# Selective scan: B and C rows repeated over the partitions by DMA instead of by TensorE, the scan's state in a PSUM bank, each product right behind its scan

## The reference, cut to what matters

```python
xn = _layer_norm(x, ln_g, ln_b)
xz = xn @ W_in.T;  u, z = xz[..., :DIN], xz[..., DIN:]
u = silu(causal_conv4(u) + conv_b)
dbc = u @ W_x.T                      # 8 columns dt_in, 16 columns B, 16 columns C
dt = softplus(dt_in @ W_dt.T + dt_bias)
dA  = exp(dt[..., None] * A)                      # decays
dBu = dt[..., None] * Bm[:, :, None, :] * u[..., None]
h = da * h + dbu;   y = einsum('bdn,bn->bd', h, c)   # for each position in turn
y = (y + u * D) * silu(z);   out = x + y @ W_out.T
```

## Time and profile before

| | |
|---|---|
| median of three runs | 1602.35 us (1600.36 to 1602.57) |
| profiled execution, its own time | 1599.76 us |
| span of its instructions | 1598.0 us |
| PE busy | 1340.2 us, 84% |
| DVE busy | 954.8 us, 60% |
| ACT busy | 699.1 us, 44% |
| POOL busy | 408.9 us, 26% |
| granted TensorE clock, mean | 0.934 of 2.4 GHz |

### The profile page before, as it was taken

The page is one execution under the profiler, slowest core; times in us unless marked ns, Lnnn a source line. Parts: engine busy times, 40 slices in busy tenths (PEclk is TensorE's granted clock), DMA queues, the critical chain, the costliest instruction groups (busy, mean ns, idle before and its releaser), DMA issues.

```text
span 1598.0 us, 24645 instructions
## 1 busy us (share of the span) xinstructions
PE 1340.2 (84%) x9074; PEld 852.2 (53%) x9127; DVE 954.8 (60%) x2239; ACT 699.1 (44%) x1988; POOL 408.9 (26%) x353
## 2 busy tenths in 40 slices
PE   7999767887887777868976468899898999999997
PEld 4666543555555433424544245555566566556664
DVE  2556667666663577685768777655674555643334
ACT  4555323456555566642645015522244555422222
POOL 1233004444431277655200224100100333400000
PEclk9999979999998889787999779999999999999999
DMA  9000000000000500000000000000000000000000
GB/s 382 1 1 1 1 1 1 1 1 1 1 1 1 212 1 1 1 0 1 2 1 0 0 0 2 1 1 0 1 2 2 1 1 1 1 1 1 0 0 13
DMA packets 4222, 25.69 MB, mean 16 GB/s; under 512 B 1168, under 2 KB 3216, under 8 KB 3472
## 3 DMA queue, kind: packets, MB, share of 16 engines
q1 hardware_dynamic: 4112, 24.24, 3.7%
HBM read 23.71 MB, written 0.52 MB: 15 GB/s over the span
## 4 chain that ended last, share of the span: by engine, by line
PE 43%; DVE 9%; issue 2%; ACT 2%; POOL 0%; DVEq 0%; ACTq 0%; POOLq 0%
PE PS L1071 6%; PE PS L641 6%; PE PS L1056 5%; PE PS L1057 5%; PE PS L707 3%; PE PS L325 2%; PE PS L357 2%; PE PS L337 2%; PE PS L298 1%; PE PS L306 1%; PE PS L1060 1%; PE PS L631 1%; PE PS L635 1%; DVE arena L877 1%; PE PS L366 1%
## 5 line engine op out<-in xcount | busy, mean ns | idle before, releaser
L549 POOL TENSOR_TENSOR arena<-arena,small 128x768 f32<-128x768 f32 (+1 forms) x64 | 107.7, 1683 | 225.3 <-DVE small L492 116.3
L877 DVE TENSOR_REDUCE arena<-PS 128x2 f32<-128x512 f32 (+1 forms) x192 | 108.9, 609 | 56.5 <-PE PS L635 55.5
L804 ACT ACTIVATE arena<-PS 128x512 f32<-128x512 f32 (+1 forms) x192 | 92.2, 532 | 109.0 <-PE PS L641 109.0
L1160 DVE TENSOR_TENSOR arena<-arena,PS 128x512 f32<-128x512 f32 x82 | 56.4, 688 | 115.9 <-ACT arena L1093 115.8
L1093 ACT ACTIVATE arena<-PS 128x512 f32<-128x512 f32 x82 | 49.0, 597 | 166.0 <-PE PS L1057 166.0
L641 PE MATMUL PS<-arena 32*128 32x256 f32 (+1 forms) x768 | 99.4, 376 | 13.6 <-DVE arena L877 9.3
L429 ACT ACTIVATE arena<-PS,small 128x256 f32<-128x256 f32 (+1 forms) x256 | 110.6, 452 | 0.0
L635 PE MATMUL PS<-arena 32*128 32x256 f32 (+1 forms) x768 | 96.6, 378 | 2.2 <-DVE arena L877 1.6
L2103 DVE TENSOR_TENSOR_SCAN arena<-PS,arena 128x512 f32<-128x512 f32 x64 | 78.1, 1222 | 27.8 <-ACT PS L2006 16.5
L2155 POOL TENSOR_TENSOR arena<-arena 128x512 f32<-128x512 f32 x64 | 80.2, 1269 | 52.6 <-ACT arena L1997 46.0
L500 DVE COPY arena<-PS 128x768 f32<-128x768 f32 (+1 forms) x64 | 69.5, 1086 | 34.5 <-PE PS L337 34.5
(11 more groups left out here) (407 smaller groups left out, 3118.4 us busy)
## 6 DMA issues: line engine op xcount, KB each, us to landing
w_last<-in_last SPq DMA_DIRECT2D x1, 8260.0 KB, 22.9
w_rest<-in_rest SPq DMA_DIRECT2D x1, 6533.5 KB, 37.2
w_last<-in_first SPq DMA_DIRECT2D x1, 4532.5 KB, 21.1
w_last<-in_first SPq DMA_DIRECT2D x1, 2176.0 KB, 10.2
X<-in_x SPq DMA_DIRECT2D x1, 512.0 KB, 4.4
CT<-in_ctxT SPq DMA_DIRECT2D x1, 512.0 KB, 10.8
out<-X SPq DMA_DIRECT2D x1, 512.0 KB, 3.2
w_consts<-in_consts SPq DMA_DIRECT2D x1, 373.0 KB, 3.1
```

The lines of the kernel that those rows point to most:

```text
L549: g.tensor_tensor(p, p, ri, ALU.mult).then_inc(self.pn_done.sem, 1)
L804: a.activation(self.PT[:, q % 8, :], PS[:, 3 + q % 3, 0:2 * n], ACT.Exp).then_inc(self.e_done.sem, 1)
L877: v.tensor_reduce(dst, src, AX.X, ALU.max, negate=True).then_inc(self.mx_done.sem, 1)
```

## The change

B and C are no longer repeated by PE. ACT's copy of dbc (now 40 rows: 32 of B and C, 8 of dt) is stored by SP to a DRAM tensor `rows`, and SP loads it back repeated over 128 partitions, two states of B and two of C in one DMA of 512 KB, into a ring of four slots in SBUF. `parts`, `spread_b`, `spread_c` and `b_copy` are gone. The banks that this frees become a fourth bank of decays (5) and the one bank of states (4). DVE does outputs(g) directly after scan(g), and scan(g) waits for outputs(g - 1). `logs` is split into `softening` (Abs, Relu, Exp; after n = 10) and `logs` (Ln; after n = 12); selections, steps, chain, gate, outputs and finish move a step or so earlier, and `dtu` has two buffers. For batch 0 the transposes of tiles 2 to 7 and their two copies come behind selections, and two table loads are issued ahead of need. The last layer's weights are loaded after the ring's last DMA. 34 products of zeros instead of 20 stand ahead of the stage. Cut to its core (declarations, the renumbered weight rows and the dropped one-hot table are left out):

```diff
-            keep_warm(self.c, pe, self.spare, 20)
+            keep_warm(self.c, pe, self.spare, 34)
...
-        return self.c.PS[:, (2, 3, 7)[g % 3], :]
+        return self.c.PS[:, (2, 3, 7, 5)[g % 4], :]
+    def state(self, g):
+        return self.c.PS[:, 4, :]
+    def spread(self, g, which):
+        return self.ring[:, g // 2 % self.RING, which * 2 + g % 2, :].unsqueeze(1).to_broadcast([P, 2, 256])
+    def out_bank(self, b):
+        return 1 if b + 1 < B else 6
...  # PE
-            if b:
-                pe.wait_ge(self.rl_ready.sem, self.rl_ready.at(0, b))
+            if b >= 2:
+                pe.wait_ge(self.z_ready.sem, self.z_ready.at(b - 2, 1))
...
-        transposes(2, 4, 5)
+        keep_warm(c, pe, 7, 3)
+        selections(0)
+        transposes(2, 4, 6)
         transposes(6, 2, 4)
-        selections(0)
-        keep_warm(c, pe, 3, 4)
         steps(0)
-        keep_warm(c, pe, 3, 16)
-        for g in range(5):
-            spread_b(g)
+        keep_warm(c, pe, 0, 24)
         for i in range(self.G):
             b, n = divmod(i, self.N)
-            spread_c(i)
             if i:
                 add(i - 1)
-            if i + 5 < self.G:
-                spread_b(i + 5)
-            if b and n == 3:
+            if b and n == 2:
                 outputs(b - 1)
...
+                if n == 6:
+                    selections(b + 1)
                 if n == 7:
-                    selections(b + 1)
-                if n == 8:
                     steps(b + 1)
...  # ACT
-            if g >= 3:
-                a.wait_ge(self.sc_ready.sem, self.sc_ready.at(0, g - 2))
+            if g >= 4:
+                a.wait_ge(self.sc_ready.sem, self.sc_ready.at(0, g - 3))
...
         silus(0)
-        normal(1, 5, 1, 2)
+        selections(0)
+        a.preload_act_table(ACT.Exp)
+        softening(0)
+        logs(0)
+        a.preload_act_table(ACT.Exp)
+        normal(1, 6, 1, 2)
         normal(2, 4, 3, 1)
-        selections(0)
-        logs(0)
-        b_copy(0)
-        b_copy(1)
         for g in range(self.G):
             decays(g)
-            if g + 2 < self.G:
-                b_copy(g + 2)
                 if n == 7:
                     silus(b + 1)
-                if n == 9:
+                if n == 8:
                     selections(b + 1)
-                if n == 11:
+                if n == 10:
+                    softening(b + 1)
+                if n == 12:
                     logs(b + 1)
...  # DVE
-            if g >= 2:
-                v.wait_ge(self.hc_ready.sem, self.hc_ready.at(0, g - 1))
-            v.tensor_tensor_scan(self.h[:, g % 2, :], self.decay(g), self.dB[:, g % 4, :], 0.0,
+            if g:
+                v.wait_ge(self.hc_ready.sem, self.hc_ready.at(0, g))
+            v.tensor_tensor_scan(self.state(g), self.decay(g), self.dB[:, g % 4, :], 0.0,
...
-            v.wait_ge(self.c_done.sem, self.c_done.at(0, g + 1))
-            v.tensor_tensor(two(self.hC[:, g % 3, :]), two(self.h[:, g % 2, :]),
-                            PS[:, 4, 0:256].unsqueeze(1).to_broadcast([P, 2, 256]), ALU.mult)\
+            v.tensor_tensor(two(self.hC[:, g % 3, :]), two(self.state(g)), self.spread(g, 1), ALU.mult)\
...
             scan(g)
-            if g:
-                outputs(g - 1)
-            if b and n == 1:
+            outputs(g)
+            if b and n == 0:
                 gate(b - 1)
-            if b and n == 4:
+            if b and n == 3:
                 finish(b - 1)
...  # POOL
-            g.wait_ge(self.bs_ready.sem, self.bs_ready.at(0, k + 1))
+            if k % 2 == 0:
+                g.wait_ge(slot.sem, slot.at(k // 2 // self.RING, 16))
...
-        self.parts(g, 0)
                 if n == 12:
-                    self.parts(g, b + 1)
-                if n == 13:
                     self.chain(g, b + 1, 0)
                     self.chain(g, b + 1, 1)
+                if n == 13:
+                    self.chain(g, b + 1, 2)
                 if n == 14:
-                    self.chain(g, b + 1, 2)
-                if n == 15:
                     self.chain(g, b + 1, 3)
                     self.chain(g, b + 1, 4)
...  # SP, ahead of the load of w_last
+    def sync(self, sp):
+        for k in range(self.G // 2):
+            b, m = divmod(k, self.N // 2)
+            if m == 0:
+                sp.wait_ge(self.dc_ev.sem, self.dc_ev.at(0, b + 1))
+                sp.dma_start(self.rows[b], self.DBC[0:32, b % 2, :]).then_inc(self.rows_out.sem, 16)
+                sp.wait_ge(self.rows_out.sem, self.rows_out.at(b, 16))
+            if k >= self.RING:
+                sp.wait_ge(self.hc_ready.sem, self.hc_ready.at(0, 2 * (k - self.RING) + 2))
+            rows = self.rows[b].rearrange("(w n) s -> w n s", w=2)[:, 2 * m:2 * m + 2, :]
+            sp.dma_start(self.ring[:, k % self.RING, :, :].rearrange("p (w n) s -> p w n s", w=2), rows.partition_broadcast(P))\
+                .then_inc(self.bc_in[k % self.RING].sem, 16)
```

More of the change, by code:

```diff
@@ L1774, with __init__ @@
     G = 16 * B
-    def __init__(self, c, g, b, win, cwb, cb, wdbc, wdt, bdt, alog, Ddiag, wout, onehot):
+    RING = 4
+    def __init__(self, c, g, b, win, cwb, cb, wdbc, wdt, bdt, alog, Ddiag, wout, rows):
         self.c, self.g, self.b, self.win, self.cb = c, g, b, win, cb
@@ L1779, in __init__ @@
         self.wdbc, self.wdt, self.bdt, self.alog, self.Ddiag = wdbc, wdt, bdt, alog, Ddiag
-        self.wout, self.onehot = wout, onehot
+        self.wout, self.rows = wout, rows
         self.x_tile = c.x_tile
@@ L1788, in __init__ @@
         self.dc_done, self.dc_ev = s("dc_done", B, 1), s("dc_ev", B, 1)
-        self.part_step = s("part_step", 7 * B, 1)
+        self.rows_out = s("rows_out", 16, B)
+        self.bc_in = [s(f"bc_in{k}", 16, len(range(k, G // 2, self.RING))) for k in range(self.RING)]
         self.dt_done, self.ab_ready, self.rl_ready = s("dt_done", B, 1), s("ab_ready", B, 1), s("rl_ready", B, 1)
@@ L1913, in tensor @@
         transposes(0, 2, 4)
-        for bank in (2, 3, 7):
+        for bank in (2, 3, 7, 5):
             keep_warm(c, pe, bank, 1)
@@ L1989, in logs @@
             a.activation(self.ex, self.ab, ACT.Exp, scale=-1.0).then_inc(self.ex_ready.sem, 1)
+        def logs(b):
             a.wait_ge(self.ex_ready.sem, self.ex_ready.at(0, b + 1))
             a.activation(self.lw, self.ex, ACT.Ln, bias=c.one, scale=1.0).then_inc(self.lw_ready.sem, 1)
[L1993 to L1997 removed]
         def decays(g):
@@ L2050, in chain @@
             eng.wait_ge(self.us_ready.sem, self.us_ready.at(0, b + 1))
-            ins = eng.tensor_tensor(self.dtu, dt, u, ALU.mult)
+            ins = eng.tensor_tensor(self.dtu[:, b % 2, :], dt, u, ALU.mult)
         ins.then_inc(self.chain_step.sem, 1)
-    def parts(self, eng, b):
-        step, full, BC, r = 7 * b, self.DBC[:, b % 2, :], self.BC[:, b % 2, :], self.rest
-        def after(ins, k):
-            ins.then_inc(self.part_step.sem, 1)
-            eng.wait_ge(self.part_step.sem, self.part_step.at(0, step + k))
-        eng.wait_ge(self.dc_ev.sem, self.dc_ev.at(0, b + 1))
-        after(eng.tensor_copy(BC[0:96], full[0:96]), 1)
-        for k in (1, 2):
-            s = slice(32 * k, 32 * k + 32)
-            after(eng.tensor_tensor(r[s], full[s], BC[s], ALU.subtract), 2 * k)
-            after(eng.tensor_copy(BC[s], r[s]), 2 * k + 1)
-        after(eng.tensor_tensor(r[64:96], r[64:96], BC[64:96], ALU.subtract), 6)
-        after(eng.tensor_copy(BC[64:96], r[64:96]), 7)
     def vector(self, v):
@@ L2122, in finish @@
             v.scalar_tensor_tensor(c.Z[:, 2 * b:2 * b + 2, :], c.X[:, 2 * b:2 * b + 2, :], 2.0,
-                                   two(PS[:, 5, 0:256]), ALU.mult, ALU.add).then_inc(self.z_ready.sem, 1)
+                                   two(PS[:, self.out_bank(b), 0:256]), ALU.mult, ALU.add).then_inc(self.z_ready.sem, 1)
         for g in range(self.G):
@@ L3069, in _ @@
             sp.dma_start(packs["rest"][:, :], dram["rest"]).then_inc(loaded["rest"], 16)
+            for s in stages:
+                if isinstance(s, Mamba):
+                    s.sync(sp)
             if "L3" in names[-1]:
@@ L3138, in program @@
             for k, a in arrays.items()}
+    dram["rows"] = nc.dram_tensor("rows", (B, 32, S), F32).ap()
     dram["out"] = nc.dram_tensor("out_0", (B * S, P), F32, kind="ExternalOutput").ap()
```

78 lines of the change are left out of this document (23 added, 55 removed).

## The result

Median 1562.51 us (1561.92 to 1563.92, four runs) against 1602.46 us of the kernel before in the same job: ratio 0.9755, interval 0.9738 to 0.9771. The gain is 40 us where 27 were forecast; the forecast's 1575 and its range from 1566 were too high. The changed kernel's profiled execution took 1562.67 us, its span 1560.9. A few executions in these jobs ran in a slower state (7017.84 us of the kernel before, 1617.00 of one experiment); the ratios leave them out.

The account below looks back on a forecast made before the run. DVE's own order was taken as the limit, with 36 us of stalls from ACT, POOL and PE. Gains of 25.5 (loop), 1.5 (start), 1.5 (end), less 1.5 (PSUM), gave 1602.35 - 27 = 1575 us; range 1566 to 1593, own range 1567 to 1583.

Parts of the forecast that it names:

- Step 1: DVE product right behind its own scan: step becomes 2.08 us (scan to product 1.26, product to scan 0.82), losing 8.8 us.
- The write to PSUM: Scan now writing its state to PSUM: bounds 0 to 6 us, 1.5 us taken off the gain.
- rival D: DVE dependence costs nothing, every pair at 1.75 us a step: 1554 us, chance 0.02.
- Steps 2 and 3: Stalls vanish: products for C 10.7 us, projection 5.8, ACT 16.5, POOL 5.6; least reserves ACT 2.6, POOL 1.2.
- Step 4: PE's adds and groups in the scan loop: lag mostly covered, 2 us of stalls charged for all batches.
- Other DVE work: DVE's gates, finishes, statistics and end tiles in the loop, beyond the steps: 6.2 us.
- Step 5: DMA ring of B and C: 11 us of latency are free, so transfers cost 0.
- Rival C: The ring feeds too slowly, at 6 us a transfer: 24 us slower, 1626 us, chance 0.06.
- The 3 to 6 us to landing: Expected sign for the ring: its transfers land in 3 to 6 us.
- Step 6: Start of the stage: first scan 1.5 us earlier, bounds 0 and 3; extra zeros put at 0.
- Step 7: End of the stage, last scan start to gate: 3.8 us in place of 5.3, gain 1.5.
- the sum itself: Loop gain 25.5, start 1.5, end 1.5, less 1.5 for PSUM: 27 us off the median 1602.35, giving 1575.

## Why the prediction was wrong, by its steps

**Step 1 held, to 0.01 us.** Scan to product is 1.27 us and product to scan 0.82, against 1.26 and 0.82. The write to PSUM, charged with 1.5 us, costs 8 ns a scan at most (1230 against 1222), 0.5 us, and is in the measured step. What the Trainium skill (VectorE: DVE Perf Modes, The DRAIN you can't avoid) says of the semaphore, that it costs nothing, isn't so here: a product that waits for the instruction directly ahead starts 0.03 us after its end, a scan 0.13, and either starts 0.08 before it where its wait is older. 1.86 against 2.09 us a step is the second of these alone, and 1.75 (rival D) was never seen, as no run had both waits older. The 4 us for PSUM, which the prediction estimated from the Trainium skill (Perfetto Trace Analysis, Optimizing Scalar/DVE Operations), aren't borne out either, by the same 8 ns.

**Steps 2 and 3 held**: all stalls behind ACT, POOL and C went. The reserves were thinner than worked out. ACT's decays for n = 8 of the first batch ended at 566.97, 0.83 us ahead of their scan at 567.80, and in the next two batches 2.5 ahead, where 2.6 was the least forecast; POOL's product for n = 15 was 0.5 us ahead in the first batch and 1.3 in the next two, where 1.2 was forecast. That three banks do as well agrees with this order of size and doesn't show a larger reserve. No run takes steps 2 and 3 apart; that each went with its own cause rests on the lists of waits.

**Step 4 was too high**: 2 us of PE stalls were charged, none over 0.2 us came. **Other DVE work** was put at 6.2 us and is 136.4 - 63 x 2.09 = 4.7: gates and finishes now stand between product and scan and take away a dependent gap of 0.2 us each. With the 1.5 of the PSUM write and 0.6 the other way for the step, the loop is 136.4 against 139.2 + 1.5.

**Step 5 held.** Rival C was worth naming: with two slots the same transfers cost 38 us. Five slots in place of four make no difference in the loop with products one behind (134.6 both). The 3 to 6 us to landing didn't hold for three of the first four transfers, nor did "no POOL wait for DMA" (one of 1.7 us, at which DVE didn't stall).

**Step 6** gave 2.6 us in place of 1.5: the zeros ahead of the inputs, put at 0, are 0.95 of it by the run with 20. **Step 7** gave 1.1 in place of 1.5.

**The step that failed is the sum itself**: "I subtract my gain from the median", with a gain made of the stage's terms alone and everything outside the stage taken as unchanged. From 1575 to 1562.5 are 12.9 us. The stage's own terms were 5.0 us too low (32.0 against 27), within their range. The 6.7 us behind the stage had no term at all, 1.7 went the other way ahead of it, and 2.9 come from setting gains between two profiled executions against a median: 5.0 + 6.7 - 1.7 + 2.9 = 12.9. Without the 6.7 the time would have been 1569, inside the range from 1566.

What the runs show in its place: the 868 us behind the stage depend on the granted clock, and a low clock in their first 40 us costs some 5 us. The profile of the kernel before had it (0.82 and 0.77 behind L848), and I read the clock only inside the scan. Of the 6.7 us, 3.5 are this and 3.2 come in later stretches.

Why the change brings the better clock stays open. It isn't the idle time of PE at the border, which is 4.06 us in both kernels. No single edit can be named: the order alone brings it (0.89 and 1.00, behind 863.2), and two of the 68 runs of the kernel before were faster by themselves (1593.47 and 1589.75 us, with mean clocks of 0.939 and 0.942 where 0.931 to 0.935 is usual), as half of those with 34 zeros were. No profile shows where in the program those executions gained.

## What to carry over

Between two DVE instructions that pass data, what costs is a wait on the one directly ahead: 0.21 us for a scan behind its product, 0.12 for a product behind its scan. A second buffer of states makes the first of these waits old and was worth 10 us here, even at the price of a bank of decays. If an operand moves to SBUF, look at what the same instruction's other operand is and what POOL does meanwhile. And when a stage is changed, read the granted clock behind its end as a term of its own: here thirteen more products of zeros in PE's idle time at the border gave the old kernel 9 us by the medians, 6.8 of them behind the stage in the profile.

## What was not expected of the hardware

- A DVE product of two SBUF operands beside a POOL product: 0.88 to 0.91 us on the mean and up to 1.51, against 0.69 with one operand in PSUM; POOL's goes from 1.27 to 1.65.
- Unchanged code behind the stage took 858.8 to 868.2 us in these kernels. The granted clock of its first 40 us accounts for up to 5.1 of that; the rest comes in later stretches, where the clock stays low for a shorter or a longer time.
- 32 DMAs that repeat 4 KB over 128 partitions, 512 KB each, leave the scan, the product and the loop as they are: loop 136.3 us without them, 136.4 with them.
